# Two graph layers on one core: the second layer's tiles in a mixed order, 31 kept tiles of x1, a ring of 63 rows

## The chip, the cores and the metric

The kernel runs on one core of a Trainium2 chip. The metric is the device time of one execution in microseconds (us); lower is better. The core's engines are called PE (TensorE), DVE (VectorE), ACT (ScalarE), POOL (GpSimd) and SP (SyncE, which only issues transfers here). Each has its own queue, runs it in the order of the program, and meets the others through semaphores.

## The reference, cut to what matters

There are 8 graphs of 2048 nodes with 256 features. The adjacency is a random 0/1 matrix with some 8 neighbours in a row.

```python
# layer 0: maximum over the first 25 neighbours, then a linear map
vals, idx = jax.lax.top_k(scores, S)                  # S = 25
feats = jax.vmap(lambda x, i: x[i])(X, idx)
agg = feats.max(axis=2)
h = jnp.concatenate([X, agg], axis=-1)
x = _layernorm(X + relu(h @ W + b))
# layer 1: attention over all neighbours, 8 heads of 32
Wh = (x @ W).reshape(Bx, Nx, H, HEAD_DIM)
e = s1[:, :, None, :] + s2[:, None, :, :] + edge_emb[edge_types]
e = jnp.where(e > 0, e, 0.2 * e)                      # masked where adj == 0
alpha = jax.nn.softmax(e, axis=2)
h = jnp.einsum('bijh,bjhd->bihd', alpha, Wh)
x = _layernorm(x + elu(layernorm(h)))
```

## The kernel before

**Tiles.** A tile is 128 nodes of one graph, so a graph has T = 16 tiles and the program 128 (`TILES`). The kernel first sorts a graph's nodes by degree, so that tile u = 0 holds the nodes with most neighbours and tile 15 those with fewest. `SLOTS` says how many neighbours a node of tile u can have: 24, 13, 12, 11, 10, 10, 9, 9, 8, 8, 7, 7, 6, 6, 5, 4. A tile with many slots is called wide here. One indirect DMA, issued by POOL, gathers one slot: 128 rows of 256 numbers in layer 0 (`sorted_d` or the input `x`) or of 264 in layer 1 (`table_d`, the rows Wh and their scores). Tile 0 packs its last slots, and the pairs of tiles (1, 2) and (5, 7) share one gather (`pair_s`), so a graph costs 141 gathers in either layer, and tile 0 costs 18.

**Rounds.** One loop of 155 rounds (`ROUNDS`) runs on every engine. In round r, layer 0 takes tile r (`tile0`, wide to narrow), and layer 1 takes its tile number j = r - 23 (`LATER` = T + 7). Which tile of the graph j stands for is said by `tile1`: in graphs 0 to 6 the places w = 0 to 15 hold tiles 15 down to 0, narrow to wide; in the last graph they hold 0 to 15. At the same time DVE searches the neighbour lists of tile r + 22 (`AHEAD`), up to round 105.

- POOL in round r: the gathers of tile r of layer 0, in graphs 0 to 2 one scatter of a table tile (`scatter_table(r - 7)`, which waits for `tab_ready`), the gathers of tile j of layer 1, and `scatter_out(j - 5)`, which waits for `final_ready`; DVE makes that in round r - 1. Every 16 rounds come 16 scatters of the sorted nodes (`scatter_lists`).
- DVE in round r: `max_tile(r)` reduces the gathered rows of layer 0 (L1140); then `steps(r)` does the searches, softmax and norms of several tiles, and ends with the product of the gathered rows of layer 1 and their weights (L1297).
- PE: `attend(j)` sums the slots of tile j, one matmul for a slot (in two pieces of the trace), after L1297; it then raises `att_ready`.
- ACT: exponentials, square roots, the table of layer 1 (L697) and copies. SP: loads, and from graph 3 on the stores of the table (`store_table`, L423).

**The ring.** The gathered rows of both layers share one buffer, `ring`, of `RING` rows. `place_tiles` gives every tile of either layer a stretch of as many rows as it has slots, in the order in which POOL gathers them, and starts again at row 0 when the next one does not fit. For every tile it notes the last earlier tile of each layer that lay in the same rows. POOL waits for their release in `gather`:

```python
need(pool, agg_ready, RING_FREE[layer, i][0])
need(pool, att_ready, RING_FREE[layer, i][1])
```

Where that function puts the tiles of layer 1 at the seam of the last two graphs is (j: slots, rows, waits for `att_ready` of): 111: 24, 13 to 36, j = 109; 112: 24, 0 to 23, j = 111; 113: 13, 24 to 36, j = 111. So j = 112 lies in rows of j = 111, the tile directly ahead of it.

**x1.** DVE writes the result of layer 0 of tile i to `x1_at(i)`, row i modulo `X1_KEPT`, in round i + 3, and reads it again in round j + 26 of the same tile. With `X1_KEPT` = 39, 39 tiles are kept.

Of the kernel before, what the change touches and what calls it, by code (L numbers as in the profile page):

```python
# [13 lines left out]
B, N, C = 8, 2048, 256  # L14
H, DH = 8, 32
T = N // P
# [45 lines left out]
DAHEAD = AHEAD + T + 3  # L62
FLAGS_AT = TILES + 2

RING = 55
X1_KEPT = 39
CONSTS0 = 2
CONSTS = 47


def tile0(i):
    return i // T, i % T


def tile1(j):
    b, w = j // T, j % T
    return b, (w if b == B - 1 else T - 1 - w)


def order_casts():  # L80
# [29 lines left out]
def place_tiles():  # L110
    at, order = 0, []
    where, before = {}, {}
    for r in range(TILES + LATER):
        for layer, i in ((0, r), (1, r - LATER)):
            if not 0 <= i < TILES:
                continue
            k = SLOTS[(tile1(i) if layer else tile0(i))[1]]
            if at + k > RING:
                at = 0
            last = [0, 0]  # L120
            for la, ib, lo, hi in order:
                if lo < at + k and at < hi:
                    last[la] = max(last[la], ib + 1)
            last[layer] = max(last[layer], i - 3)
            where[layer, i], before[layer, i] = at, tuple(last)
            order.append((layer, i, at, at + k))
            at += k
    return where, before
# [5 lines left out]
def pair_of(layer, i):  # L134

    u = (tile1(i) if layer else tile0(i))[1]
    for c, pair in enumerate(PAIRS):
        if u in pair:
            there = [k for k in range(i - i % T, i) if (tile1(k) if layer else tile0(k))[1] in pair]
            return c, pair.index(u), bool(there)  # L140
    return None
# [17 lines left out]
def build(nc, x, adj, w0, b0, w1, a1, a2, emb, gamma, beta, out):  # L159
    ctx = ExitStack()  # L160
    with ctx:
        def sb(name, shape, dt=F32):
            return ctx.enter_context(nc.sbuf_tensor(name, shape, dt))
# [44 lines left out]
        has = sb("has", [P, 6])  # L208
        ring = sb("ring", [P, RING * ROW])
        xs = [sb(f"xs{q}", [P, C]) for q in range(4)]  # L210
        agg = [sb(f"agg{q}", [P, C]) for q in range(2)]
        h_t = [sb(f"h_t{q}", [P, 2 * C]) for q in range(2)]
        z0 = sb("z0", [P, C])
        x1k = sb("x1k", [P, X1_KEPT * C])
        x1_t = [sb(f"x1_t{q}", [P, C]) for q in range(2)]
# [167 lines left out]
        def x1_at(i):  # L383
            return x1k[:, i % X1_KEPT * C:(i % X1_KEPT + 1) * C]

# [28 lines left out]
        def _(sp):  # L414
            def load_adj(k):
                q, n = k % 2, CASTS[k][1]
                need(sp, cast_done, k - 1)
                sp.dma_start(adj_i[q][:, :], adj_rows[n * P:(n + 1) * P, :]).then_inc(adj_ld[q], 16)
# [22 lines left out]
            def load_pay(g):  # L441
                need(sp, list_out, 16 * T * g)
                sp.dma_start(pay[:, :].rearrange("p (t k) -> p t k", k=SENT)[:, :, 0:C],
                             x_rows[g * N:(g + 1) * N, :].rearrange("(t p) c -> p t c", p=P)).then_inc(pay_ld, 16)
# [16 lines left out]
            for n in range(2, 8):  # L461
                load_adj(n)
            sp.wait_ge(consts_done, CONSTS)
            load_pay(0)
# [47 lines left out]
        def _(pool):  # L512
# [37 lines left out]
            for c in range(4):  # L550
# [4 lines left out]
                                    fill=0.0, base=0, pattern=[[1, P]], channel_multiplier=-1))  # L555
            assert steps == CONSTS

# [241 lines left out]
        def _(pe):  # L799
            def totals(g):  # L800
                pe.wait_ge(onehot_ready, SORTS.index(g) + 1)
                for c in range(4):
                    last = pe.matmul(turn_p[:, c:c + 1], onehot[:, P * c:P * (c + 1)], ones_h[:, 0:1],
                                     start=True, stop=True)
                last.then_inc(tot_ready, 1)
# [72 lines left out]

            pe.wait_ge(consts_done, CONSTS)
            totals(0)  # L880
# [93 lines left out]
        def _(dve):  # L974
# [45 lines left out]
            def search(n):  # L1020
                t = n % T
                settle()
                mark(n)
                settle()
                chunks(n)
                settle()
                top_lists(cand[:, :], lambda r: lists[:, t * WORDS + 8 * r:t * WORDS + 8 * r + 8], WIDEST // 8)

            def degree_codes(g):
                settle()  # L1030
                if g >= RANKED:
                    dve.wait_ge(cast_done, CAST_AT["degree", g * T + T - 1] + 1)
                v.tensor_scalar(degc[:, :], degree[:, g * T:(g + 1) * T], float(DCODE - 1), None, ALU.min)
                settle()
                v.tensor_tensor(onehot[:, :].rearrange("p (d t) -> p d t", t=T),
                                degc[:, :].unsqueeze(1).broadcast_to([P, DCODE, T]),
                                drev[:, :].unsqueeze(2).broadcast_to([P, DCODE, T]), ALU.is_equal)\
                    .then_inc(onehot_ready, 1)
# [268 lines left out]
            for n in range(T):  # L1307
                search(n)
            dve.wait_ge(consts_done, CONSTS)
            degree_codes(0)  # L1310
# [155 lines left out]
```

## Time and profile before

| | us |
|---|---|
| median of 3 runs | 3435.09 (3434.9 to 3439.38) |
| the profiled execution | 3435.9 |
| its span, first to last instruction | 3434.2 |
| POOL busy | 2484.3 (72%) |
| DVE busy | 2417.8 (70%) |
| PE busy | 1578.9 (46%) |
| ACT busy | 1114.7 (32%) |

No engine is busy for more than three quarters of the span. A busy share leaves out what an engine spends between its instructions, and it averages over stages; so the waits, and the gaps between instructions of one engine, have to be read beside it.

### The profile page before, as it was taken

The page shows a single profiled execution, that of the slowest core. Times are in us where ns is not written, and L with a number is a line of the kernel's source. Part 1 is how long each engine was busy: PE and PEld are TensorE (multiplying, and loading weights), DVE is VectorE, ACT ScalarE, POOL GpSimd, SP SyncE. Part 2 cuts the span into 40 slices and gives each one's busy share as a digit, 9 for nine tenths or more (in the row PEclk, how much of TensorE's full clock was granted, in tenths as well). Part 3 has the DMA queues.
Part 4 walks back from the last instruction along what each step waited for, and adds up shares of the span by engine and source line. Part 5 has one row for each costly group of instructions (what it writes and reads, how often), then busy time and mean ns, then how long its engine had stood idle before and what let it go on. Part 6 is the DMA issues. An engine that isn't in the chain of part 4 may idle for free. (4 is left out here: it accounts for less than half of the span.)

```text
span 3434.2 us, 25542 instructions
## 1 busy us (share of the span) xinstructions
PE 1578.9 (46%) x5123; PEld 1176.3 (34%) x5131; DVE 2417.8 (70%) x5791; ACT 1114.7 (32%) x2307; POOL 2484.3 (72%) x2612
## 2 busy tenths in 40 slices
PE   0036455433563445544365344544454444654354
PEld 0024234322442333333244333433343333443333
DVE  8798789575776767777697766967675545655466
ACT  3224345332343333433344333422222221332134
POOL 2476777777777777777777777777777777777575
PEclk9986667656666666667676676666666666777676
DMA  6657777755576555766568555565544444444232
GB/s 233 215 193 243 260 261 235 227 173 181 174 235 210 183 185 188 249 201 198 173 215 263 187 189 173 179 186 152 152 117 123 115 116 115 120 117 112 74 106 76
DMA packets 221587, 610.01 MB, mean 178 GB/s; under 512 B 68849, under 2 KB 112882, under 8 KB 194802
## 3 DMA queue, kind: packets, MB, share of 16 engines
q0 software_dynamic: 122880, 342.62, 33.6%
q1 hardware_dynamic: 98546, 265.71, 22.7%
q14 instruction: 117, 0.96, 0.1%
q8 instruction: 44, 0.72, 0.1%
HBM read 555.19 MB, written 52.95 MB: 177 GB/s over the span
## 5 line engine op out<-in xcount | busy, mean ns | idle before, releaser
L585 POOL DMA_INDIRECT ring<-table_d,idx_loc x1096 | 1050.3, 958 | 362.6 <-issue 361.4
L585 POOL DMA_INDIRECT ring<-sorted_d,idx_cur x685 | 658.7, 962 | 210.1 <-issue 209.2
L847 PE MATMUL score_p<-ident,x1k 128*128 128x128 f32 x256 | 81.1, 418 | 1406.3 <-ACT x_t L685 1402.5
L875 PE MATMUL att_p<-ring,ident 128*128 128x256 f32 (+1 forms) x2384 | 608.3, 414 | 176.1 <-DVE ring L1297 175.4
L1140 DVE TENSOR_REDUCE agg<-ring 128x256 f32<-128x2560 f32 (+9 forms) x120 | 453.7, 3781 | 207.4 <-DMA ring<-sorted_d,idx_cur 145.2
L875 PEld LDWEIGHTS att_p<-ring,ident 128*128 128x128 f32 (+1 forms) x2384 | 500.7, 212 | 279.4 <-DVE ring L1297 153.2
L847 PEld LDWEIGHTS score_p<-ident,x1k 128*128 128x128 f32 x256 | 35.9, 197 | 1457.0 <-issue 1452.4
L716 ACT ACTIVATE neg<-z 128x256 f32<-128x256 f32 x128 | 53.3, 416 | 1397.9 <-DVE z L1183 1397.9
L585 POOL DMA_INDIRECT ring<-in_x_dram,idx_cur x411 | 392.2, 954 | 130.8 <-issue 124.6
L839 PE MATMUL lin_p<-w_s,h_t 128*128 128x256 f32 x1024 | 471.5, 641 | 0.0
L839 PEld LDWEIGHTS lin_p<-w_s,h_t 128*128 128x128 f32 x1024 | 319.6, 327 | 149.0 <-issue 81.1
L1017 DVE MAX8 cand<-adj_h 128x8 f32<-128x256 bf16 x1024 | 345.5, 408 | 1.6
L1297 DVE TENSOR_TENSOR ring<-ring,score_p 128x2048 f32<-128x2048 f32 (+10 forms) x128 | 320.6, 2504 | 10.1 <-issue 0.7
L562 POOL DMA_INDIRECT sorted_d<-pay,rank_i x128 | 123.8, 967 | 123.9 <-DVE rank_i L1048 85.2
L855 PE MATMUL wh_p<-w_s,x_t 128*128 128x272 f32 x512 | 190.6, 509 | 20.4 <-ACT self_s L697 20.4
L665 ACT ACTIVATE adj_h<-adj_i 128x2048 bf16<-128x2048 int32 x48 | 91.7, 1909 | 283.5 <-DVE cand L1017 241.2
L1119 DVE COPY ring<-pair_s 64x264 f32<-64x264 f32 (+1 forms) x64 | 20.8, 325 | 217.8 <-DMA pair_s<-table_d,pair_loc 78.2
L611 POOL DMA_INDIRECT out_dram<-res,own_out x128 | 128.2, 1001 | 60.9 <-issue 36.2
L1111 DVE COPY ring<-ring 32x512 f32<-32x512 f32 (+1 forms) x48 | 22.1, 461 | 210.8 <-DMA ring<-table_d,top_loc 126.4
L722 ACT ACT_TABLE_LOAD x132 | 169.4, 1283 | 2.3
L1013 DVE TENSOR_TENSOR adj_h<-adj_h,score_p 128x2048 bf16<-128x2048 bf16 x128 | 154.4, 1206 | 19.5 <-ACT adj_h L665 16.5
L718 ACT ACT_TABLE_LOAD x128 | 164.2, 1283 | 7.2 <-issue 0.7
(159 smaller groups left out, 2850.8 us busy)
## 6 DMA issues: line engine op xcount, KB each, us to landing
adj_i<-in_adj_dram SPq DMA_DIRECT2D x208, 1024.0 KB, 5.8
ring<-table_d,idx_loc POOLq DMA_INDIRECT x1096, 2.8
pay<-in_x_dram SPq DMA_DIRECT2D x8, 2048.0 KB, 9.8
xs<-sorted_d SPq DMA_DIRECT2D x128, 128.0 KB, 5.7
ring<-sorted_d,idx_cur POOLq DMA_INDIRECT x685
table_d<-tab SPq DMA_DIRECT2D x80, 132.0 KB, 3.8
ring<-in_x_dram,idx_cur POOLq DMA_INDIRECT x411
sorted_d<-pay,rank_i POOLq DMA_INDIRECT x128, 3.6
```

The source lines that it names most:

```text
L562: pool.indirect_dma_start(out=sorted_d[g], out_offset=bass.IndirectOffsetOnAxis(ap=rank_i[g % 2][:, t:t + 1], axis=0), in_=pay[:, t * SENT ...
L585: pool.indirect_dma_start(out=to[:, k * width:(k + 1) * width], out_offset=None, in_=source, in_offset=bass.IndirectOffsetOnAxis(ap=idx_at ...
L611: pool.indirect_dma_start(out=out_rows, out_offset=bass.IndirectOffsetOnAxis(ap=own_out[:, b * T + u:b * T + u + 1], axis=0), in_=res[j % ...
L718: act.activation(neg[:, :], neg[:, :], ACT.Exp, scale=-1.0).then_inc(elu_ready, 1)
L722: act.activation(std[:, :], var[:, :], ACT.Sqrt).then_inc(std_ready, 1)
L839: last = pe.matmul(lin_p[:, 0:C], h_t[i % 2][:, P * c:P * (c + 1)], w0_s[:, c, :], start=False, stop=(c == 3))
L855: last = pe.matmul(wh_p[:, 0:ROW + H], x1_t[i % 2][:, P * c:P * (c + 1)], w1_s[:, c, :], start=(c == 0), stop=(c == 1))
L875: last = pe.matmul(att_p[:, 0:C], ident[0:on, :], r3[0:on, s, 0:C], start=(s == 0), stop=(s == k - 1))
L1013: v.tensor_tensor(adj_h[n % 2][:, :], adj_h[n % 2][:, :], code_p, ALU.mult)
L1017: last = v.max(cand[:, 8 * c:8 * c + 8], adj_h[n % 2][:, CH * c:CH * (c + 1)])
L1140: last = v.tensor_reduce(a, rows.rearrange("p (k c) -> p c k", c=C), AX, ALU.max)
L1297: v.tensor_tensor(g4[:, 0:w], g4[:, 0:w], p3[:, 0:w, :].unsqueeze(3) .broadcast_to([P, w, H, DH]), ALU.mult).then_inc(weighted, 1)
```

## The change

It changes three tables and no work. `ORDER1` says which tile stands at which place of layer 1 in graphs 0 to 6: the tile widths at places 0 to 15 become 9, 5, 7, 24, 12, 10, 6, 4, 13, 11, 10, 8, 7, 9, 8, 6. The last graph keeps its order 0 to 15. A tile's place is at most 7 behind its number, so x1 has to be kept for fewer tiles: `X1_KEPT` falls from 39 to 31, which frees 8 x 256 numbers in a partition, and `RING` grows by 8 rows of 264, from 55 to 63. The ring's places and its waits are worked out anew by the same function.

```diff
-RING = 55
-X1_KEPT = 39
+RING = 63
+X1_KEPT = 31
...
+ORDER1 = [6, 14, 11, 0, 2, 4, 13, 15, 1, 3, 5, 8, 10, 7, 9, 12]
...
 def tile1(j):
     b, w = j // T, j % T
-    return b, (w if b == B - 1 else T - 1 - w)
+    return b, (w if b == B - 1 else ORDER1[w])
```

At the seam the tiles of layer 1 now lie (j: slots, rows, waits for `att_ready` of): 111: 6, 8 to 13, j = 107; 112: 24, 14 to 37, j = 108; 113: 13, 38 to 50, j = 109. Each waits for a tile four places ahead of it. In the graphs before, the gather of layer 0 in round 64, which waited for j = 39 of round 62, now waits for j = 38 of round 61. Two tiles of layer 1 wait for the 24-slot tile two places ahead of them: j = 21 in round 44 (for j = 19) and j = 37 in round 60 (for j = 35); everywhere else a gather that needs the rows of a 24-slot tile comes at least three rounds after it.

On POOL, at the seam between graph 6 and graph 7 (`table_d6` and `table_d7`), the order before was:

```order
L585 DMA ring<-table_d6,idx_loc0 128x264 x11
L595 DMA pair_s1<-table_d6,pair_loc0 128x264
L611 DMA out_dram<-res0,own_out 16384x256
L585 DMA ring<-table_d6,idx_loc0 128x264 x12
L611 DMA out_dram<-res1,own_out 16384x256
L585 DMA ring<-table_d6,idx_loc0 128x264 x16
L585 DMA ring<-table_d6,top_loc0 128x264 x2
L611 DMA out_dram<-res2,own_out 16384x256
L585 DMA ring<-table_d7,idx_loc1 128x264 x16
L585 DMA ring<-table_d7,top_loc1 128x264 x2
L611 DMA out_dram<-res3,own_out 16384x256
```

and now it is:

```order
L590 DMA ring<-table_d6,idx_loc0 128x264 x8
L616 DMA out_dram<-res0,own_out 16384x256
L590 DMA ring<-table_d6,idx_loc0 128x264 x8
L616 DMA out_dram<-res1,own_out 16384x256
L590 DMA ring<-table_d6,idx_loc0 128x264 x6
L616 DMA out_dram<-res2,own_out 16384x256
L590 DMA ring<-table_d7,idx_loc1 128x264 x16
L590 DMA ring<-table_d7,top_loc1 128x264 x2
L616 DMA out_dram<-res3,own_out 16384x256
```

The two 18-gather tiles no longer follow each other; the last tile of graph 6 has 6 gathers.

On PE, the same seam: L875 (L880 now) is `attend`, L862 (L867) the mean of the last graph. Before:

```order
L875 MATMUL att_p<-ring,ident 128x256 x10
L855 MATMUL wh_p<-w_s,x_t 128x272 x2
L875 MATMUL att_p<-ring,ident 128x256 x60
L862 MATMUL turn_p<-w_s,xmean 128x256 x2
L875 MATMUL att_p<-ring,ident 128x256 x149
```

Now:

```order
L880 MATMUL att_p<-ring,ident 128x256 x8
L860 MATMUL wh_p<-w_s,x_t 128x272 x2
L880 MATMUL att_p<-ring,ident 128x256 x30
L867 MATMUL turn_p<-w_s,xmean 128x256 x2
L880 MATMUL att_p<-ring,ident 128x256 x149
```

Of the slots of graph 6 that are left behind the last table tile, there were 60 (11, 12, 13 and 24) and now there are 30 (7, 9, 8 and 6).

On POOL, in graph 2, the 24-slot tile now stands at place 3, and what comes between it and the tile that waits for its rows (the 10 gathers from `table_d2` at the end, j = 37) is:

```order
L590 DMA ring<-table_d2,idx_loc2 128x264 x16
L590 DMA ring<-table_d2,top_loc2 128x264 x2
L616 DMA out_dram<-res2,own_out 16384x256
L590 DMA ring<-sorted_d3,idx_cur1 128x256 x7
L590 DMA ring<-table_d2,idx_loc2 128x264 x11
L600 DMA pair_s1<-table_d2,pair_loc2 128x264
L616 DMA out_dram<-res3,own_out 16384x256
L590 DMA ring<-sorted_d3,idx_cur1 128x256 x6
L590 DMA ring<-table_d2,idx_loc2 128x264 x10
```

Before, this stretch of rounds held the narrow tiles of 6, 6 and 7 slots.

## Rows read from the trace of the kernel before

**Rows 1.** The groups of POOL's instructions: busy us, mean ns, idle before.

```profile
L585 POOL DMA_INDIRECT ring<-table_d,idx_loc x1096 | 1050.3, 958 | 362.6 <-issue 361.4 <-PE att_p L875 1.2
L585 POOL DMA_INDIRECT ring<-sorted_d,idx_cur x685 | 658.7, 962 | 210.1 <-issue 209.2 <-PE att_p L875 0.3 <-DVE agg L1135 0.3
L585 POOL DMA_INDIRECT ring<-in_x_dram,idx_cur x411 | 392.2, 954 | 130.8 <-issue 124.6 <-DMA top_cur<-sorted_d 5.9 <-DVE agg L1135 0.3
```

**Rows 2.** POOL's waits: us in total, times, the longest.

```profile
POOL ring L585 <- issue: 705.0, 2217, 28.4
POOL sorted_d L562 <- DVE rank_i L1048: 85.2, 1, 85.2
POOL out_dram L611 <- DVE res L981: 24.6, 9, 6.7
POOL table_d L604 <- ACT self_s L697: 21.3, 6, 8.6
```

**Rows 3.** Stretches: length, then busy us (instructions) of PE, PEld, DVE, ACT, POOL.

```profile
404.00:3062.00 2658.00, 1291.75 (x4266) 967.33 (x4272) 1881.43 (x4440) 879.60 (x1870) 2017.67 (x2098) 0.67 0.58 182
3174.00:3203.00 29.00, 14.69 (x52) 11.53 (x52) 14.73 (x28) 4.21 (x7) 0.57 (x2) 0.66 0.02 6
3203.00:3401.00 198.00, 90.29 (x280) 70.43 (x280) 117.48 (x309) 59.89 (x103) 150.47 (x157) 0.71 0.38 106
```

**Rows 4.** POOL in order of time, at its three waits for the ring.

```profile
1491.97 0.96 POOL L585 DMA_INDIRECT ring<-sorted_d,idx_cur  x1 [1.78 <-issue]
...
3150.47 1.08 POOL L585 DMA_INDIRECT ring<-table_d,idx_loc  x1 [0.85 <-PE att_p L875]
...
3202.62 0.96 POOL L585 DMA_INDIRECT ring<-table_d,idx_loc  x1 [28.43 <-issue]
```

**Rows 5.** PE in order of time, the attend steps at those waits.

```profile
1487.32 3.62 PE L875 MATMUL att_p<-ring,ident 128*128 128x256 f32 x16
...
3188.25 13.62 PE L875 MATMUL att_p<-ring,ident 128*128 128x256 f32 x48 [21.25 <-DVE ring L1297]
```

**Rows 6.** POOL, PE and DVE in order of time, around one 24-slot tile.

```profile
2101.84 0.95 POOL L585 DMA_INDIRECT ring<-table_d,top_loc  x1 [0.30 <-issue]
...
2116.23 4.42 DVE L1297 TENSOR_TENSOR ring<-ring,score_p 128x4096 f32<-128x4096 f32 x1
...
2120.70 10.82 PE L875 MATMUL att_p<-ring,ident 128*128 128x256 f32 x48 [2.42 <-DVE ring L1297]
```

**Rows 7.** PE in order of time, the slowest attend of 24 slots.

```profile
1324.15 14.57 PE L875 MATMUL att_p<-ring,ident 128*128 128x256 f32 x48 [3.19 <-DVE ring L1297]
```

**Rows 8.** Two stretches of the attend at 3188: PE busy (pieces) first; PEclk third from last.

```profile
3188.00:3191.00 3.00, 2.75 (x7) 2.21 (x8) 2.31 (x8) 1.69 (x2) 0.00 (x0) 0.50 0.00 0
3194.00:3197.00 3.00, 3.00 (x16) 2.64 (x15) 0.00 (x0) 0.00 (x0) 0.00 (x0) 1.00 0.00 0
```

**Rows 9.** DVE and POOL in order of time, a result and its scatter in narrow rounds.

```profile
2191.29 0.41 DVE L981 TENSOR_SCALAR res<-y,mv,rstd 128x256 f32<-128x256 f32 x1
...
2194.07 1.00 POOL L611 DMA_INDIRECT out_dram<-res,own_out  x1 [0.30 <-issue]
```

**Rows 10.** Busy us (and instructions) again, seven rounds and the five after them.

```profile
1889.60:2104.10 214.50, 84.67 (x288) 65.12 (x288) 143.21 (x317) 67.10 (x129) 162.99 (x170) 0.65 0.60 188
2104.10:2195.10 91.00, 51.81 (x186) 37.82 (x187) 80.39 (x205) 31.21 (x68) 69.35 (x71) 0.71 0.53 162
```

**Rows 11.** DVE's groups by shape, two widths of L1297.

```profile
L1297 DVE TENSOR_TENSOR ring<-ring,score_p 128x2560 f32<-128x2560 f32 x16 | 45.1, 2821 | 1.2
L1297 DVE TENSOR_TENSOR ring<-ring,score_p 128x2304 f32<-128x2304 f32 x16 | 40.9, 2554 | 1.2
```

**Rows 12.** ACT in order of time: the last table tile is ready.

```profile
3138.72 0.17 ACT L697 ACTIVATE self_s<-wh_p 128x8 f32<-128x8 f32 x1
```

**Rows 13.** The page's DMA issues: KB each, us from issue to landing.

```profile
table_d<-tab SPq DMA_DIRECT2D x80, 132.0 KB, 3.8
```

**Rows 14.** L585 by kind: duration ns min/median/max, first and last start.

```profile
L585 POOL DMA_INDIRECT ring<-table_d,idx_loc x1096: 942/946/1297, 489.1 to 3399.3; - x183
```

## The prediction

> **What bounds the kernel now.** I read the waits first, since the page's busy shares name no engine. In the order of time POOL issues one gather after another. A gather takes 0.959 us on average (2,101 us over 2,192) [rows 1], and nearly every one is preceded by a gap that ends for nothing the profile shows: 705.0 us over 2,217 gathers [rows 2], two long ones of them (28.43 and 1.78 [rows 4]); the rest are 0.305 us each. A gather thus costs POOL 1.264 us, and the 72% of the page stand for an engine that is never free. The stretches say the same: 2,098 instructions from 404 to 3062 times 1.264 are 2,652 of 2,658 us, and the 157 after 3203 are all of 198 us [rows 3]. DVE is busy for 1,881 of those 2,658 us [rows 3] and waits mostly for gathered rows.
>
> The program has 2,560 indirect DMAs on POOL behind the start: 128 scatters of sorted nodes, 8 x 2 x 141 = 2,256 gathers, 48 scatters of tables, 128 of results. At 1.264 us they make 3,236 us. The start adds 111 us, 85.2 of them the wait for the first ranks [rows 2], and the profiled span is 3434.2. What is left, 87 us, is almost all waits on POOL. They are: 19 us for table tiles in the first graph (21.3 less six gaps of 0.3) [rows 2]; some 22 us at the very end, where POOL has only results to send and waits for DVE (24.6 less nine gaps) [rows 2]; 5.6 us for the first index lists [rows 1]; the last transfer; and three waits for the ring. Those three are the part that the change can reach.
>
> **The waits for the ring.** At 3202.62 POOL has sat idle for 28.43 us [rows 4]. The profile puts it under "issue". Counted back along the order from the end, POOL ended the 18 gathers of j = 111 (tile 0 of graph 6) and a result before the gap, and starts the 18 of j = 112 (tile 0 of graph 7) after it. j = 112 lies in the rows of j = 111, so it waits for `att_ready` of that tile, and PE's attend of 24 slots runs from 3188.25 for 13.62 us, to 3201.87, 0.75 us before POOL goes on [rows 5]. From 3174 to 3203 POOL has two instructions [rows 3]. The same wait, small, stands at 3150.47 (0.85 us, put down to PE) and at 1491.97 (1.78 us, also under "issue") [rows 4]; the attend of j = 39 ended at 1490.94 [rows 5]. Less the usual 0.30 us the three are 28.13 + 0.55 + 1.48 = 30.2 us.
>
> **The change, part by part.**
> *Number of instructions.* No gather, scatter or matmul is added or taken away. POOL's 3,226 us stay.
> *The seam.* j = 112 now waits for j = 108, a tile of 7 slots, and between the two lie tiles of 8, 8 and 6 gathers and four results: 26 issues, 32.9 us. A 24-slot tile's rows were free at most 33.4 us after its last gather (below), one of 7 slots is some 10 us quicker. So the wait of 28.13 us goes, and the next condition in line is the table of graph 7. Its last tile was ready at 3138.9 [rows 12]. POOL had ended the gathers of that round, 132, two results and 12 gathers, 17.7 us, ahead of 3149.6 [rows 4], at 3131.9; so the table is ready 7.0 us behind round 132's gathers and lands 3.8 us later [rows 13]. Now 17 issues, 21.5 us, lie there before j = 112; 21.5 - 7.0 - 3.8 leaves 10.7 us. So: -28.1 us.
> *The two small waits.* j = 111 now waits for a tile four rounds back, round 64 for one three rounds back: -0.55 and -1.48.
> *The 24-slot tile at place 3.* Here a new wait can come. From the end of its last gather to the end of its L1297 it took 2120.65 - 2102.79 = 17.9 us, and then PE took 10.8 us [rows 6], in the slowest case 14.6 [rows 7], 13.6 at the seam [rows 5]. With 0.9 us until POOL answers, its rows are free 29.6 to 33.4 us after its last gather. The tile that waits two rounds later comes after 1 result, 7 gathers, 12 gathers, 1 result and 6 gathers, 27 issues, 34.1 us, in graph 2 (round 60), and two table scatters, 2.5 us, later in graph 1 (round 44). Margin 0.7 to 4.5 us. Everywhere else 11 issues more, 13.9 us, lie between. I take 0; the far bound is a wait at both places.
> The engine's clock matters there. In the attend at the seam PE finished 7 pieces in 3 us at a granted clock of 0.50, the lower level (1.2 GHz), after it had sat idle, and 16 in 3 us at 1.00 (2.4 GHz) [rows 8]. All 48 pieces at the lower rate would take about 48 / 2.7 = 18 us, 3.4 us more than the slowest, and POOL would wait 3 us at round 60 and 0 to 1 at round 44. The Trainium skill, page "TensorE: Matmul & The Clock Gate", section "What's actually happening", says that a gate halves the array's clock until it has been busy for a while; by that rule a wide tile always begins at the lower level, as the row shows, and it speaks against the change only where another gather waits closely behind, so for 4 us at most.
> *Wide beside wide.* Over layer 0's wide rounds (0 to 6 of a graph) POOL has 170 issues before and 147 now, and over the next five 71 before and 94 now; the sum of a graph is the same. DVE was busy for 143 of 214.5 us in the first seven, and for 80.4 of 91 in the five where it hardly waited [rows 10]. Its own gaps at that rate would be 143 x 10.6 / 80.4 = 19 us, so it waited about 52 us for POOL. POOL now needs 23 x 1.26 = 29 us less there, DVE 30 slots x 0.267 = 8 us less (2,821 and 2,554 ns for 10 and 9 slots [rows 11]); 52 - 29 + 8 leaves 31 us of slack. In the other five rounds POOL gets 29 us more and DVE 29 x 0.267 = 8. POOL stays the bound in both, and moving work between them gives 0. The narrow rounds were the closest before: a result was ready at 2191.70 and was sent at 2194.07 [rows 9], 2.4 us later. That spot gets wider.
> *The first graph and the tail.* The table waits of the start lie before round 16, where layer 1 has not begun and layer 0 keeps its order: 0. The last graph keeps its order, its tiles wait for tiles four rounds back before and after: 0.
> *Sum.* 3434.2 - 30.2 = 3404.0 us of span. The profiled execution took 3435.9 us, 1.7 more than its span and 0.8 more than the median; on the median that is 3435.1 - 30.2 = 3404.9, with 0 to 4 us for the wide tile. I say **3405.5**.
>
> **The rivals.**
> *A part of the stall comes back.* The margins of 10.7 us (table) and 0.7 to 4.5 us (place 3) are taken from durations of one execution. If both fail by some microseconds, or DVE arrives later at them, 5 to 15 us return: 3410 to 3420. For it: the margins are small against 28 us. Against: places with 2.4 us of margin held before.
> *The stall is not what I think, or something else fills it.* If POOL's 28 us had another cause the time stays at 3433 to 3437. A mechanism that would fill it is a slower gather: the mean of 958, 962 and 954 ns lies above the median of 946 [rows 1, 14], 27.6 us in all over the 2,192 of [rows 1]; some gathers take up to 1,297 ns. If this excess doubled because POOL now works beside other instructions of DVE, it would eat the gain: 3433. The Trainium skill, page "SBUF — State Buffer", section "SBUF: two separate sides", says that a DVE copy of the kind L1119 is can hold a port which POOL needs to write its descriptors; by that rule a gather beside a copy is the slow one, which no row here shows or denies. DVE has as many copies as before, so I expect the same excess.
> *Slower.* The wide tile at place 3 comes into the rounds in which DVE also sorts and makes the lists (DVE busy for 80.4 of 91 us [rows 10]), and leaves the ring late in each of the seven graphs, with POOL standing behind it and layer 0's next wide tile queued behind that. To lose more than is won it has to cost 30.2 / 7 = 4.3 us a graph. In five graphs the margin is 14.6 us or more, so DVE and PE together would have to be 19 us later than in [rows 7], a DVE part of 37 instead of 18 us; at 10 us of wait in each graph, 7 x 10 - 30.2 gives 3475. Nothing in the rows points there.
>
> **How the numbers follow.** Full gain 0.80 (3402 to 3409); part of it 0.11 (3410 to 3420); nothing left 0.05; slower 0.04. The range 3400 to 3415 leaves out the last two and half of the second, and its low end allows for a few of the 22 us of waits that I count as fixed. Two runs of this kernel can be told apart from about 0.2%, 7 us: below 3428 is faster. Faster 0.91, same 0.05, slower 0.04.
>
> **What would show it.** POOL's gaps under "issue" before gathers fall from 705 to about 675 us with a longest of a few us; POOL's row at the start of graph 7 has a gap of 0.3 us. The waits for table tiles (21 us) and for results at the end (25 us) stay. DVE's waits for gathered rows fall by about 28 us, most of it at the first tile of the last graph. The mean of a gather stays at 959 ns. I am wrong if a long gap stands at POOL's gathers in rounds 44 or 60, at the first gather of graph 7 for the table, or if POOL's results in rounds 128 to 134 wait for DVE.

## The result: 25 us less

The changed kernel took 3412.2 us (median of four runs, 3409.9 to 3413.6), the kernel before 3437.24 (four runs, 3434.9 to 3440.9). The ratio is 0.9925, with a 95% interval of 0.9913 to 0.9936: 25 us less, between 22 and 30. The prediction said 3405.5 and 3400 to 3415. The profiled execution took 3413.55 us, 1.7 more than its span. In the runs further below, the medians of runs 1, 5 and 11 include one execution each in a slower state (4161, 4134 and 3693 us), which the ratios and intervals leave out.

The first lines of its page, the span and the engines' busy time:

```profile
span 3411.9 us, 25547 instructions
...
PE 1586.7 (47%) x5123; PEld 1178.9 (35%) x5131; DVE 2417.1 (71%) x5791; ACT 1113.9 (33%) x2307; POOL 2487.7 (73%) x2612
```

Before, the span was 3434.2 with as many instructions on each of these engines. Work was not removed; waiting was. POOL's waits, which answer to [rows 2] (us in total, times, the longest):

```profile
POOL ring L590 <- issue: 675.7, 2218, 0.3
POOL sorted_d L567 <- DVE rank_i L1053: 85.3, 1, 85.3
...
POOL out_dram L616 <- DVE res L986: 24.9, 11, 6.7
POOL table_d L609 <- ACT self_s L702: 22.4, 6, 8.6
```

Only the first differs by much: 705.0 us with a longest gap of 28.4 became 675.7 us with a longest of 0.3. No gap before a gather that the profile puts under "issue" is longer now than the usual 0.30 us. POOL in order of time at the seam, where [rows 4] has the gap of 28.43 us (start, us, then what it is, and the idle time ahead of it):

```profile
3173.97 0.94 POOL L590 DMA_INDIRECT ring<-table_d,idx_loc  x1 [0.30 <-issue]
3175.21 1.00 POOL L616 DMA_INDIRECT out_dram<-res,own_out  x1 [0.30 <-issue]
3176.52 0.96 POOL L590 DMA_INDIRECT ring<-table_d,idx_loc  x1 [0.30 <-issue]
```

The gather at 3176.52 is the first of j = 112. It stood at 3202.62 before. The stretch from 3174 to 3203 that held two instructions of POOL [rows 3] now holds 23:

```profile
404.00:3062.00 2658.00, 1292.88 (x4258) 966.41 (x4264) 1875.35 (x4402) 869.10 (x1846) 2019.44 (x2097) 0.67 0.58 182
3174.00:3203.00 29.00, 10.43 (x32) 8.03 (x32) 11.59 (x34) 6.20 (x10) 22.11 (x23) 0.68 0.38 107
```

The columns are those of [rows 3]. The first row shows the other half of the story: in the long middle of the program POOL does 2,097 instructions in 2,658 us, before 2,098. POOL's pace there did not change with the mixing of wide and narrow tiles.

**The account.** From the last rows of the two timelines the last result is issued 26.0 us earlier (3402.90 against 3428.87). The predicted 30.2 us of ring waits are all gone. Of them POOL gave back 1.1 in waits for table tiles (22.4 against 21.3 [rows 2]) and 3.4 in longer instructions (2487.7 us busy against 2484.3), which leaves 25.7. Behind that last issue the program needs another 9.0 us, before 5.3; so the span shrank by 22.3 only. The last issue before and now:

```profile
3428.87 0.96 POOL L611 DMA_INDIRECT out_dram<-res,own_out  x1 [4.18 <-DVE res L981]
```

```profile
3402.90 0.96 POOL L616 DMA_INDIRECT out_dram<-res,own_out  x1 [3.83 <-DVE res L986]
```

This last difference is no scatter. In all nine traces of kernels with the new order and 31 kept tiles (this one and runs 1, 4, 6, 7, 8, 10, 11 and 12) the span ends 8.9 to 9.0 us behind the last issue, with the ring of 55 rows too (run 4); in the five with the old order everywhere but in graph 6 (before and runs 2, 3, 5 and 9) it ends 5.0 to 5.6 us behind it. So 3 to 4 us of the seam's gain are given back at the very end. What takes them no run shows.

### The profile page after: what moved, and what is told of

It reads as the page before. It is cut to its first block, busy times and chain, and to the rows that moved or that the text cites. A ratio compares the mean times of both kernels' runs of the same rounds, so it can differ in the third digit from the quotient of the medians.

```text
span 3411.9 us, 25547 instructions
## 1 busy us (share of the span) xinstructions
PE 1586.7 (47%) x5123; PEld 1178.9 (35%) x5131; DVE 2417.1 (71%) x5791; ACT 1113.9 (33%) x2307; POOL 2487.7 (73%) x2612
## 4 chain that ended last, share of the span: by engine, by line
POOL 66%; issue 22%; DVE 7%; DMA 1%; DVEq 1%; ACT 1%; PE 1%; SPq 0%; POOLq 0%; ACTq 0%
POOL ring L590 57%; POOL sorted_d L567 4%; POOL out_dram L616 4%; DVE cand L1022 2%; DVE agg L1145 2%; POOL table_d L609 1%; DVEq L983 1%; POOL pair_s L600 1%; DVE adj_h L1018 1%; DMA adj_i<-in_adj_dram 0%; DVE lists L1006 0%; DMA ring<-sorted_d,idx_cur 0%; PE lin_p L844 0%; DVE agg L1135 0%; DMA pair_s<-sorted_d,pair_cur 0%
## 5 line engine op out<-in xcount | busy, mean ns | idle before, releaser
L590 POOL DMA_INDIRECT ring<-table_d,idx_loc x1096 | 1047.6, 956 | 333.9 <-issue 333.3
L590 POOL DMA_INDIRECT ring<-sorted_d,idx_cur x685 | 659.5, 963 | 208.7 <-issue 208.4
L880 PE MATMUL att_p<-ring,ident 128*128 128x256 f32 (+1 forms) x2384 | 602.4, 411 | 138.6 <-DVE ring L1302 138.0
L880 PEld LDWEIGHTS att_p<-ring,ident 128*128 128x128 f32 (+1 forms) x2384 | 497.4, 210 | 242.0 <-DVE ring L1302 126.7
L590 POOL DMA_INDIRECT ring<-in_x_dram,idx_cur x411 | 395.3, 962 | 130.8 <-issue 124.3
L1302 DVE TENSOR_TENSOR ring<-ring,score_p 128x1536 f32<-128x1536 f32 (+10 forms) x128 | 320.6, 2505 | 10.5 <-issue 1.2
L860 PE MATMUL wh_p<-w_s,x_t 128*128 128x272 f32 x512 | 199.1, 527 | 17.5 <-ACT self_s L702 17.2
L1124 DVE COPY ring<-pair_s 64x256 f32<-64x256 f32 (+1 forms) x64 | 19.9, 311 | 221.5 <-DMA ring<-table_d,idx_loc 62.2
L860 PEld LDWEIGHTS wh_p<-w_s,x_t 128*128 128x128 f32 x512 | 143.2, 283 | 64.1 <-issue 24.5
```

What stands on the lines that cost most here:

```text
L590: pool.indirect_dma_start(out=to[:, k * width:(k + 1) * width], out_offset=None, in_=source, in_offset=bass.IndirectOffsetOnAxis(ap=idx_at ...
L860: last = pe.matmul(wh_p[:, 0:ROW + H], x1_t[i % 2][:, P * c:P * (c + 1)], w1_s[:, c, :], start=(c == 0), stop=(c == 1))
L880: last = pe.matmul(att_p[:, 0:C], ident[0:on, :], r3[0:on, s, 0:C], start=(s == 0), stop=(s == k - 1))
L1302: v.tensor_tensor(g4[:, 0:w], g4[:, 0:w], p3[:, 0:w, :].unsqueeze(3) .broadcast_to([P, w, H, DH]), ALU.mult).then_inc(weighted, 1)
```

## The experiments

Runs 1 to 8 were on two chips on which both kernels take some 20% longer (the kernel before 4119.5 on one and 4136.7 us on the other), and runs 9 to 12 on chips like that of the result (3443.4 for runs 9 and 10, 3438.5 for 11 and 12). The first chip had runs 1 to 4, the second runs 5 to 8. Ratios are always to the kernel before on the same chip. Theory A, B and the rivals are those that the expectations name.

### 1. The changed kernel as it is (e0_after)

> The changed kernel, timed beside the kernel before on one chip. Three waits of POOL for the ring, 30.2 us in all, are gone from its trace, but the first timing gave 25.0 us less (ratio 0.9925, interval 0.9913 to 0.9936), and the profiled spans differ by 22.3. Theory A (the gain is the waits, the rest of the difference is scatter and somewhat longer issues on POOL): 25 to 31 us less. Theory B (the new order costs something of its own, 3 to 5 us, everywhere in the program): 22 to 27 us less.

4077.7 us, ratio 0.9893 (0.9854 to 0.9933). On this chip DVE is busy for the same time (2413.3 us) and the span is 4057.8. POOL's waits are of another kind:

```profile
POOL ring L590 <- issue: 664.7, 2176, 1.2
POOL out_dram L616 <- DVE res L986: 279.9, 36, 23.0
POOL ring L590 <- remote: 197.3, 39, 10.0
POOL table_d L609 <- ACT self_s L702: 163.4, 19, 21.1
```

POOL waits for results and for table tiles, which come late from DVE and ACT. Of the chain of work that ended last the page gives POOL 12% and DVE 32% here, against 66% and 7% in the profile of the result. So what holds for this chip need not hold for the one of the result, and the main comparisons were made again later.

### 2. and 3. Only the seam, whole and by half (e1_seam_clear, e2_seam_half)

The kernel before with one reordered graph: rows, x1 and all other graphs as they were. In run 2 tile 0 of graph 6 stands two places earlier, in run 3 one place.

```diff
+ORDER6 = [15, 14, 13, 12, 11, 10, 9, 8, 7, 6, 5, 4, 3, 0, 2, 1]
...
-    return b, (w if b == B - 1 else T - 1 - w)
+    return b, (w if b == B - 1 else ORDER6[w] if b == B - 2 else T - 1 - w)
```

`...` stands for lines left out. For run 3 the list ends in 3, 2, 0, 1.

> The kernel before with the ring of 55 rows, 39 kept tiles and its own order in graphs 0 to 5 and 7; in graph 6 alone the 24-slot tile stands at place 13 instead of 15 (13, 12, 24 becomes 24, 12, 13 slots at the end, nearly). The first tile of the last graph then waits for a tile of graph 6 three places ahead. Theory A (only the wait at the seam mattered): POOL's gap of 28.4 us becomes 0.3, the small one of 1.8 us at round 64 stays, and the time falls by 27 to 30 us, as much as by the whole change or 1 us less. Rival C (mixing wide and narrow tiles in every graph evens out the rounds and that brings the gain): one graph of seven is touched, and at its end only, so 0 to 5 us less.

> As the run before, but the 24-slot tile of graph 6 stands at place 14, one place before the end. The first tile of the last graph then waits for the 24-slot tile two places ahead, with 13 gathers and two results (some 18 us of POOL) between them. Theory A: of the 28.1 us of wait 12 to 14 us are left, and the time falls by 14 to 17 us, half as much. Rival C: 0 to 5 us less, as in the run before.

Whole: 4095.5 us, ratio 0.9938 (0.9913 to 0.9963). By half: 4106.1, ratio 0.9978 (0.9962 to 0.9994). The further the two 18-gather tiles stand apart, the less time: 9 us and then 26 (expected: 14 to 17 and 27 to 30). The trace of run 3 shows the wait itself. PE's attend of the 24-slot tile ends at 3838.98, and POOL goes on 0.74 us later, as at the seam before (0.75); the idle time is now 12.03 us, where 12 to 14 were expected:

```profile
3825.49 13.49 PE L878 MATMUL att_p<-ring,ident 128*128 128x256 f32 x48 [25.63 <-issue]
```

```profile
3839.72 0.96 POOL L588 DMA_INDIRECT ring<-table_d,idx_loc  x1 [12.03 <-issue]
```

In run 2 it is 4.97 us there, and 5.19 in run 5, where 0.3 was expected. That the whole change gives more here (0.9893) spoke for a second source of gain.

### 4. The small ring in the changed kernel (e3_ring55)

```diff
-RING = 63
+RING = 55
```

> The changed kernel with its order and 31 kept tiles, but a ring of 55 rows. The first tile of the last graph still waits for one that is long done. What differs is the lag of the other waits: j = 3, the 24-slot tile of graph 0, lies in rows of layer 0's tile 25 of the round before, and j = 5 in those of j = 3. Theory A with the margins of the prediction: POOL waits there once or twice in rounds 26 to 28, 5 to 9 us, and up to 3 us at rounds 76 and 92, so the time lies 5 to 11 us above the changed kernel. Rival D (the 63 rows do nothing that the order does not do): the same time as the changed kernel within 3 us.

4074.3 us, ratio 0.9897 (0.9868 to 0.9927), 2 us above run 1. The two intervals leave some 20 us either way, so the 5 to 11 us of theory A are not excluded; only the greater part of the 44 us that the whole change gives on this chip is not due to the eight rows. In the traces POOL waits longer for `attend` with the small ring (89.9 us in 11 places against 53.6 in 4) and shorter for results (222.3 against 279.9). On the other kind of chip it was not tried.

### 5. The seam once more (e4_seam_clear2)

The kernel of run 2, on the second chip.

> The kernel that clears the seam alone (graph 6 with its 24-slot tile at place 13, all else as before), once more, since on the chip of the first four runs every engine had stops of its own that the first profiles do not have (4119 us for the kernel before instead of 3437). On a chip like the first: theory A, 27 to 30 us less than before (POOL's gap at the seam gone and nothing else moved); theory B (the order of the whole change costs 3 to 5 us of its own) expects this run to be 2 to 5 us faster than the changed kernel; rival C (mixing in all graphs brings the gain) 0 to 5 us less than before.

4104.5 us, ratio 0.9909 (0.9874 to 0.9943). With run 2 the seam alone is worth 26 to 38 us there, and its interval meets that of the whole change. The second source was no longer sure. The changed kernel itself was not timed on the second chip.

### 6. Fewer instructions on POOL (e5_less_out)

The changed kernel without the result scatters of graphs 1 to 4, 64 of the 128; those rows of the output are not written.

```diff
+def sent(j):
+    return not T <= j < 5 * T
...
+                if not sent(j):
+                    return
```

Left out of this cut are the waits for earlier scatters, on SP and DVE, which count the 64 fewer.

> The changed kernel without the scatters of results of graphs 1 to 4: 64 indirect DMAs of POOL are left out, and those rows of the output are not written. They stand in rounds 44 to 107. Theory A (POOL's issues set the pace there): 64 times 1.30 us, 80 to 84 us less than the changed kernel. Rival (DVE or the transfers set the pace, POOL's issue slots are slack): 0 to 15 us less.

4000.3 us, ratio 0.9665 (0.9641 to 0.9689). Against the changed kernel, whose ratio is that of run 1 on the first chip, this is 0.0228 x 4137 = 94 us, 1.5 for each scatter, with some 19 us of uncertainty either way from the intervals alone. The 80 to 84 us of theory A lie within it, the 0 to 15 of the rival do not. A scatter left out takes its wait for the result with it, and POOL's waits for results are long on this kind of chip (279.9 us in run 1, 98.5 here), so this run does not say how much of the time is the issue and how much the wait.

### 7. and 12. More work on DVE (e6_dve_more, e11_dve_more2)

The changed kernel with four of the eight maxima of a tile taken twice in rounds 32 and up, which adds 296 instructions, and a `settle()`, in which DVE waits for its own last results, in each of these rounds.

```diff
+                    if r >= 32:
+                        for c in range(4):
+                            v.max(cand[:, 8 * c:8 * c + 8], adj_h[n % 2][:, CH * c:CH * (c + 1)])
+                        settle()
```

> The changed kernel with four of the eight maxima of L1017 done twice in rounds 32 to 105, 74 rounds: 1.35 us more work on DVE a round, 100 us in all, with one more drain. No result changes. Theory A (DVE waits for POOL some 50 us a graph in the wide rounds, and POOL sets the pace): 0 to 5 us more than the changed kernel. Rival (the two engines take turns as the bound): 30 to 100 us more.

> The changed kernel with four of the eight maxima of L1017 done twice in rounds 32 to 105, 100 us more work on DVE in all, for a chip without stops of the engines. Theory A (there DVE waits for POOL some 50 us a graph, and POOL sets the pace): 0 to 5 us more than the changed kernel. Rival (the engines take turns as the bound): 30 us or more. On a chip with stops: some 55 us more, as before.

Run 7, on the second chip: 4147.8 us, ratio 1.0027 (1.0008 to 1.0047), 0.0134 x 4137 = 55 us more than the changed kernel (again with the ratio of run 1, from the other chip, and some 18 us of uncertainty). Theory A missed there; the rival's 30 to 100 us hold. Run 12, on a chip like that of the result: 3413.1 us, ratio 0.9926 (0.9914 to 0.9939), against 0.9927 for the changed kernel beside it. The page of run 12 on the engines, and then what was added (busy us, mean ns):

```profile
PE 1585.8 (46%) x5123; PEld 1178.5 (35%) x5131; DVE 2526.0 (74%) x6087; ACT 1113.5 (33%) x2307; POOL 2486.6 (73%) x2612
```

```profile
L1185 DVE MAX8 cand<-adj_h 128x8 f32<-128x256 bf16 x296 | 103.4, 410 | 0.0
```

103.4 us more on an engine that is busy for longer than POOL (2526.0 against 2486.6 us) cost nothing that the intervals, some 6 us either way, let one see. POOL's gaps stayed at 0.30 us:

```profile
POOL ring L590 <- issue: 676.3, 2219, 0.3
```

DVE took the time out of its waits: for transfers they add up to 639 us, in the profiled execution of the result to 754. This is the clearest evidence on what sets the pace in rounds 32 to 105, and it speaks against a gain from the evening out of rounds, which could only have come from DVE's side. At the start (85 us of waiting for ranks) and at the very end POOL does wait for DVE, and there nothing was added.

### 8. and 10. The table scatters a round later (e7_lag8, e9_lag8b)

The changed kernel, in which POOL scatters a table tile one round later, except the last of a graph. Table tiles were the largest wait left in the middle of POOL's work.

```diff
-                if first(r - LAG0) and (r - LAG0) // T < RANKED:
-                    scatter_table(r - LAG0)
+                for i in range(RANKED * T):
+                    if r == i + (LAG0 if i % T == T - 1 else LAG0 + 1):
+                        scatter_table(i)
```

> The changed kernel with the table scatters of POOL one round later (tile r - 8 instead of r - 7 in round r, but the last tile of a graph stays where it is, so the two last ones go together). POOL waited 22 us for table tiles in rounds 7 to 15 of the first graph, 8.6 us the longest. Theory A (any wait of POOL that goes is time won): the waits go, but a wait of up to 7 us for the ranks of graph 1 takes the place of a part, 8 to 17 us less than the changed kernel. Rival (in rounds 7 to 27 DVE is the bound, never starved, and POOL only runs into the next wait): 0 to 4 us less.

> The changed kernel with the table scatters one round later, again, for a chip like the first. There, theory A: 8 to 17 us less than the changed kernel, near 3400; the rival (DVE is the bound up to round 27): 0 to 4 us less, near 3410. On a chip like the second: no gain over the changed kernel, as before, since POOL there waits for DVE's results in other places (36 to 45 times) and only moves its wait.

Run 8: 4107.3 us, ratio 0.9941 (0.9917 to 0.9965); the gain of theory A did not come there. By the ratio of run 1, from the other chip, it is 20 us slower, with as much uncertainty. POOL waits longer for results instead (367.2 us). Run 10: 3403.5 us (3402.7 to 3404.7), ratio 0.9885 (0.9869 to 0.9902), 40 us below the kernel before; it is the best of all versions that write the whole output. Its waits:

```profile
POOL ring L590 <- issue: 675.3, 2215, 0.3
POOL sorted_d L567 <- DVE rank_i L1054: 85.9, 2, 85.2
...
POOL ring L590 <- DMA top_cur<-sorted_d: 7.8, 2, 5.8
POOL table_d L609 <- ACT self_s L703: 6.1, 1, 6.1
```

The six waits for table tiles (22.4 us) became one of 6.1; the waits for index lists and ranks grew by 2.5. That is 13.8 us less of waiting. Against the changed kernel of run 11 the ratios give 0.0042 x 3438 = 14 us. Within the 7 us that the two intervals leave, a microsecond of waiting taken from POOL is a microsecond of the kernel.

### 9. Only the seam, on a chip like that of the result (e8_seam_clear3)

The kernel of run 2.

> The kernel that clears the seam alone, a third time, in the hope of a chip like the first. On such a chip (before near 3437 us, DVE's gaps without a cause some 11 us in all): theory A, 27 to 30 us less than before and POOL's gap at the seam 0.3 us. Theory B, the order of the whole change costs 3 to 5 us of its own, wants it at 3407 to 3409 against the 3412.2 of the changed kernel. Rival C 0 to 5 us less than before. On a chip like the second (before near 4120 to 4137): 25 to 32 us less, as the two runs so far.

3415.2 us (3414.0 to 3417.1), ratio 0.9919 (0.9902 to 0.9935): 28.3 us less. POOL's waits for the ring, and the small one that this edit leaves:

```profile
POOL ring L588 <- issue: 676.9, 2216, 1.7
```

Three tiles in another place give all that the whole change gives. The long gap is gone, the 1.7 us at round 64 is still there. The 0.85 us at 3150.47 [rows 4] went with the long one, so 28.7 us of waiting were taken away for the 28.3 gained.

### 11. The changed kernel on the chip of run 12 (e10_after2)

> The changed kernel beside the kernel before, for a chip without stops of the engines. Theory A (the seam alone brings the gain, the order nothing): the ratio of the seam run, 0.9919, within 2 us. Theory B (the order of the whole change costs a few us of its own, in longer scatters and gathers of POOL): 3 to 5 us above that, a ratio of 0.993 or a little less, as in the first timing (0.9925).

3415.6 us, ratio 0.9927 (0.9914 to 0.9940). It repeats the result (0.9925) on another chip. It lies between theory A (0.9919) and theory B (0.993), and its interval holds both.

## Why the prediction was right

**What bounds the kernel.** The argument was that POOL, 72% busy, is never free, since each instruction costs its 0.96 us and 0.30 us more. Run 12 bears it out from one side (103 us of DVE are free), run 10 from the other (14 us of POOL's waits are some 14 us of the kernel). The 3,226 us that the change was said to leave are the 3,236 of the paragraph before, 2,560 times 1.264; nothing hangs on the difference.

**The cause of the 28 us.** The profile put that gap under "issue", and the prediction put it down to the attend of the 24-slot tile 0.75 us ahead of its end [rows 4, 5]. Run 9 takes away this dependence and no instruction, and the gap goes, with 28.3 us. The first rival was that the gap had another cause; it fell. In the half-way order of run 3 the gap was 12.03 us and again ended 0.74 us behind the attend of the 24-slot tile, so the wait shrinks with the distance between the two tiles. In time run 3 gave a third of run 2's gain (the intervals allow up to more than half).

**The two small waits.** Predicted -0.55 and -1.48. Both stand at 0.30 in the trace of after; the second is the one that run 9 keeps. Together with the seam, POOL's idle time ahead of the three groups of [rows 1] fell from 703.5 to 673.4 us (333.9, 208.7 and 130.8, in the rows further below): 30.1, where 30.2 was summed.

**The table margin at the seam, 10.7 us.** ACT in order of time, where the last table tile is ready, which answers to [rows 12], and the issue-to-landing time of the page ([rows 13]):

```profile
3161.34 0.17 ACT L702 ACTIVATE self_s<-wh_p 128x8 f32<-128x8 f32 x1
```

```profile
table_d<-tab SPq DMA_DIRECT2D x80, 132.0 KB, 3.9
```

It lands at about 3161.5 + 3.9 = 3165.4, and POOL could begin at 3176.22: 10.8 us of margin. The part that this rests on, how far the tile is ready behind the gathers of round 132, came out at 6.9 us (they end at 3154.6) where 7.0 was taken.

**The 24-slot tile at place 3.** The margin was put at 0.7 to 4.5 us. In rounds 58 and 60, first the last gather of the wide tile and the tile that needs its rows, then PE's attend between them:

```profile
1403.16 0.95 POOL L590 DMA_INDIRECT ring<-table_d,top_loc  x1 [0.30 <-issue]
...
1438.52 0.95 POOL L590 DMA_INDIRECT ring<-table_d,idx_loc  x1 [0.30 <-issue]
```

```profile
1422.46 12.51 PE L880 MATMUL att_p<-ring,ident 128*128 128x256 f32 x48 [2.54 <-DVE ring L1302]
```

The attend ends at 1434.97; with 0.9 us until POOL answers and 1438.22 as the time at which POOL is ready, 2.4 us were left. This is the middle of the forecast. At round 44 5.0 us were left by the same count. Had the attend taken the 18 us that were worked out for the lower clock, POOL would have waited some 3 us. (The 18 us stand for 8 pieces in 3 us; the 7 pieces in 2.75 busy us of [rows 8] give 19.) The clock in two stretches of it (the granted clock is the third value from the end):

```profile
1422.50:1425.50 3.00, 3.00 (x9) 2.42 (x10) 3.00 (x2) 0.00 (x0) 2.39 (x3) 0.59 0.53 166
1429.00:1432.00 3.00, 3.00 (x14) 2.37 (x13) 2.01 (x9) 2.40 (x4) 2.36 (x3) 1.00 0.35 114
```

It begins near the lower level, behind an idle stretch of 2.54 us, and 6.5 us later it is at the higher one. The rule of the Trainium skill, page "TensorE: Matmul & The Clock Gate", section "What's actually happening", that the array runs at half its clock until it has been busy for a while, agrees with these two rows; it costs the tile's first pieces and not all 48. But the prediction went too far with its "always begins at the lower level": the attend of [rows 6], idle for 2.42 us ahead of it, had the higher level and 14 pieces in its first 3 us:

```profile
2120.70:2123.70 3.00, 3.00 (x14) 2.66 (x15) 2.91 (x3) 0.00 (x0) 2.09 (x4) 1.00 0.61 210
```

**Wide beside wide.** The prediction gave this 0. In the trace POOL's last instruction of rounds 47, 63 and so on up to 127, the last of each graph, is 31 to 33 us later than before, since 23 gathers (29 us) of layer 1 come earlier in each graph. No wait grows from it, and it is given back in the first seven rounds of the next graph, whose layer 1 tiles are the narrower for it (at the end of round 54 POOL is 4.2 us later than before; at the end of round 134, the last of these, 2.0 us later, where the sum has it 2.0 earlier; behind the seam, at the end of round 135, 25.9 us earlier). That reading would be wrong only if DVE's slack were used up; run 12 shows some 100 us of it in rounds 32 to 105.

**What was off.** The point was 6.7 us too low: 3412.2 lies in the band of the rival in which a part of the stall comes back (3410 to 3420) and not in that of the full gain (3402 to 3409), though the stall was gone in full. So the range held, with the right mechanism, by its width. 2.1 us of the 6.7 are the kernel before, whose median of four executions is 3437.2 and not 3435.1. The rest are terms that were put at nothing. In the spans, 3404.0 was forecast and 3411.9 measured; three terms, of 3.4, 1.1 and 3.7 us, make up this difference within 0.3.

First, "POOL's 3,226 us stay": POOL was busy 3.4 us longer. The groups that answer to [rows 1]:

```profile
L590 POOL DMA_INDIRECT ring<-table_d,idx_loc x1096 | 1047.6, 956 | 333.9 <-issue 333.3
L590 POOL DMA_INDIRECT ring<-sorted_d,idx_cur x685 | 659.5, 963 | 208.7 <-issue 208.4
...
L590 POOL DMA_INDIRECT ring<-in_x_dram,idx_cur x411 | 395.3, 962 | 130.8 <-issue 124.3
...
L616 POOL DMA_INDIRECT out_dram<-res,own_out x128 | 130.7, 1021 | 60.5 <-issue 35.6
```

The mean of a gather did stay at 959 ns: these gathers together rose by 1.2 us only (2102.4 against 2101.2), and results by 2.5. I had expected 0 of both. Is it the new order? Results took a mean of 1,022 ns in run 11, 1,018 in run 12 and 1,020 in run 10, all with the new order, and 1,004 in run 9 and 1,001 before with the old one; that speaks for it. On the slower chips they took 1,000 to 1,005 ns with either order. And POOL's busy time does not speak for it: 2,488.0, 2,486.6 and 2,489.2 us with the new order, and 2,484.3 and 2,492.1 with the old. It varies by 8 us without a change of order, and the ratios of run 9 (0.9919) and of the changed kernel (0.9925, 0.9927) lie within each other's intervals. So a cost of the new order of some 2 us for results is possible and not shown. Second, the waits for table tiles were said to stay at 21 us and came to 22.4 (23.4 and 22.2 in runs 11 and 12, and 21.2 in run 9 with the old order of tiles). Third, the end: "the last transfer" was counted as fixed, and the stretch behind the last issue took 9.0 us and not 5.3. This one goes with the whole change in every trace (8.9 to 9.0 us in nine, 5.0 to 5.6 in the other five), so theory B, that the whole change costs 3 to 5 us of its own, is right in the traces by this much, though at one place and not everywhere. The timings (0.9919 in run 9; 0.9925 and 0.9927) fit it and cannot settle it. Why the stretch is longer stays open.

**The other rivals.** Gathers that slow down beside DVE's copies: in the two timelines, the gathers that overlap one of DVE's copies inside the ring (L1111, L1119, L1120) take 981 and 980 ns on average (107 before, 110 after) and the others 959. That is 2 us in the whole kernel, the same before and after. Beside the kind that the prediction names, L1119, they take 963 and 965 ns; beside L1111, which unpacks the widest tile, 1,026 and 1,020 (30 and 32 gathers). The rule of the Trainium skill, page "SBUF — State Buffer", section "SBUF: two separate sides", that such a copy can hold the port which POOL needs, thus shows here at most as some 5 ns a gather beside L1119 and some 65 beside L1111; the copies are few, and 0.3 to 0.5 us long. The slower case, a wide tile late by 10 us in each graph, had nothing in the traces.

**A sign that I misread.** DVE's waits for gathered rows were to fall by 28 us. All its waits for transfers fell from 772 to 754, 18 us. The wait at the seam's first tile itself fell by 20.7 us, from 36.2 to

```profile
3200.84 1.50 DVE L1116 COPY ring<-ring 32x528 f32<-32x528 f32 x3 [15.47 <-DMA ring<-table_d,top_loc]
```

and DVE waited longer in other places. A sum over an engine that has slack is a poor measure of what the critical engine gained.

## What to carry to other kernels

An engine that issues small indirect DMAs one after another can be the bound at 72% busy: add the fixed gap between two instructions to their duration before comparing engines, and then count only that engine's waits. Look for its one long gap at the joint of two phases, count back through the buffer order to whose rows are being waited for, and try the smallest reordering first; here three tiles gave what the whole new order gave. Before an order is changed for the sake of evenness, see whether the evened engine is the one that sets the pace. And compare what lies behind the last instruction of the critical engine: here 3 to 4 us of the gain went there.

## What the runs showed of the hardware

**On two chips the engines paused between instructions.** On the chips of runs 1 to 8 the kernel before took 4119 and 4137 us and not 3437. DVE's and POOL's durations were the same: DVE 2413.3 us in all for 5,791 instructions (2417.1 on the other kind), a gather from the tables 956 ns on both. PE was busy for longer, 1678.7 against 1586.7 us, at a mean granted clock of 0.66 against 0.69. What differs most are gaps: DVE had 1330 us of gaps in 565 places put down to nothing that the profile shows or to "remote", against 13 us in 37 places. DVE in order of time in run 1:

```profile
2012.39 0.42 DVE L1254 SCALAR_TENSOR_TENSOR y<-z,neg 128x256 f32<-128x256 f32 x1
2017.01 0.42 DVE L1263 SCALAR_TENSOR_TENSOR z<-lin_p,xs 128x256 f32<-128x256 f32 x1 [4.20 <-issue]
...
2021.20 0.43 DVE L1272 BATCH_NORM_STATS2 stats<-z 128x6 f32<-128x256 f32 x1 [3.11 <-issue]
...
2028.21 0.17 DVE L1288 TENSOR_SCALAR var<-mv 128x3 f32<-128x3 f32 x1 [3.06 <-issue]
```

Pauses of 3 to 4 us stand ahead of ordinary short instructions. Why, no run here shows, nor whether it belongs to the chip or to the hour, since each chip was used once. The consequence is shown, with the uncertainty said above: DVE's work costs time there (55 us for about 100) and moving a table scatter gains nothing, whereas on the other kind it is the reverse. A comparison holds for the kind of chip on which it was made; the same kernel's ratio was 0.9893 on one and 0.9925 and 0.9927 on the other.

**Matmul pace.** The same attend of 48 pieces took 10.8, 13.6 and 14.6 us before [rows 5 to 7] and 12.5 in the place looked at after. What differs is how long PE stays at the lower level: the one of 10.8 us had the higher from its start, the one of 14.6 [rows 7] the lower (0.50) in two stretches of 3 us, with 7 and 8 pieces, and then 15 pieces in 3 us at 0.99. So a single row of such a step is no price for it, and a margin has to be set against the longest.
